# Sampling of a transformer block: one PSUM bank for the takes of both head blocks, output products in halves, another order at the end of the weight stage

## What is computed

```python
v = (value @ w_value + b_value)            # 16 heads of 16
off = (query @ w_off + b_off)              # 4 points of 2 coordinates per head and token
attw = softmax(query @ w_attw + b_attw)    # weights of the 4 points
sx = clip(off[..., 0], 0.0, 1.0); ix = ((sx + 1.0) * L - 1.0) * 0.5
x0 = floor(ix); fx = ix - x0               # between two neighbours of v
sampled = v[x0] * (1 - fx) * ... + v[x0 + 1] * fx * ...
out = einsum('bhlpd,bhlp->blhd', sampled, attw)
x = x + out @ w_out + b_out
```

## Time and profile before

| | us |
|---|---|
| median of 3 runs | 1006.85 |
| lowest, highest | 1002.65, 1007.42 |
| the profiled execution, its own time | 1004.41 |
| its span | 1002.6 |
| mean granted TensorE clock in it | 0.932 of full speed |

### The profile page before, as it was taken

The page is one execution under the profiler, slowest core; times in us unless marked ns, Lnnn a source line. Parts: engine busy times, 40 slices in busy tenths (PEclk is TensorE's granted clock), DMA queues, the critical chain, the costliest instruction groups (busy, mean ns, idle before and its releaser), DMA issues.

```text
span 1002.6 us, 12939 instructions
## 1 busy us (share of the span) xinstructions
PE 838.5 (84%) x4501; PEld 539.6 (54%) x4501; DVE 684.9 (68%) x1237; ACT 539.4 (54%) x1009; POOL 306.0 (31%) x236
## 2 busy tenths in 40 slices
PE   4999998799999998788888899599998994005998
PEld 3776675577777886244444444344443441004887
DVE  2567767866775676579888888735534999895333
ACT  2444434455334665666666666134428995982432
POOL 2100000566110222587777778200010431000000
PEclk9999999799999999599999999799998997556999
DMA  9800000010000000000000000000002436710111
GB/s 290 256 1 1 1 1 1 0 55 0 2 11 1 1 1 1 0 2 1 1 1 1 2 1 2 1 0 1 0 1 84 168 146 275 262 71 11 53 52 53
DMA packets 23446, 45.41 MB, mean 45 GB/s; under 512 B 2323, under 2 KB 18646, under 8 KB 22230
## 3 DMA queue, kind: packets, MB, share of 16 engines
q1 hardware_dynamic: 21776, 43.08, 12.1%
q10 hardware_dynamic: 1606, 1.52, 0.5%
HBM read 27.80 MB, written 16.78 MB: 44 GB/s over the span
## 4 chain that ended last, share of the span: by engine, by line
PE 60%; DVE 20%; POOL 8%; ACT 6%; issue 5%; ACTq 1%; DMA 0%; DVEq 0%; POOLq 0%
PE pair L1313 8%; PE pair L1272 8%; POOL hat L596 5%; PE pair L967 5%; PE pair L1194 4%; PE pair L1075 3%; PE pair L1102 3%; PE pair L1208 3%; PE pair L971 3%; DVE peak L1758 2%; DVE wide L1753 2%; DVE peak L1743 2%; DVE wide L1781 2%; PE pair L1012 2%; PE pair L1104 2%
## 5 line engine op out<-in xcount | busy, mean ns | idle before, releaser
L596 POOL TENSOR_TENSOR hat<-hat 128x1024 f32<-128x1024 f32 x62 | 145.6, 2360 | 45.1 <-DVE hat L1619 44.4
L1178 PE MATMUL pair<-rows,sel 32*128 32x512 bf16 x256 | 75.4, 397 | 23.1 <-ACT down_b L816 17.3
L1619 DVE SCALAR_TENSOR_TENSOR hat<-pair,down_a 128x1024 f32<-128x1024 f32 x64 | 78.1, 1220 | 21.8 <-PE pair L1170 19.7
L1297 PE MATMUL pair<-xqs,wuT 128*128 128x512 f32 x192 | 85.9, 610 | 4.8 <-ACT up_stage L861 4.8
L816 ACT ACTIVATE down_b<-pair 128x512 f32<-128x512 f32 x128 | 69.4, 595 | 37.0 <-PE pair L1178 32.1
L816 ACT ACTIVATE down_a<-pair 128x512 f32<-128x512 f32 x128 | 69.5, 595 | 33.5 <-PE pair L1178 24.0
L1313 PE MATMUL pair<-wdT,hid 128*128 128x256 f32 x384 | 84.8, 384 | 2.9 <-DVE hid L1800 2.9
L1619 DVE SCALAR_TENSOR_TENSOR hat<-pair,down_b 128x1024 f32<-128x1024 f32 x64 | 78.0, 1219 | 11.9 <-PE pair L1170 11.7
L1272 PE MATMUL pair<-xqs,wgT 128*128 128x512 f32 x192 | 85.1, 601 | 0.0
L1313 PEld LDWEIGHTS pair<-wdT,hid 128*128 128x128 f32 x384 | 74.1, 193 | 13.5 <-DVE hid L1800 3.2
L513 POOL TENSOR_TENSOR rstd<-lnt,half 128x8 f32<-128x8 f32 (+2 forms) x15 | 26.5, 1769 | 167.5 <-DVE lnt L1354 167.5
(11 more groups left out here) (208 smaller groups left out, 1880.8 us busy)
## 6 DMA issues: line engine op xcount, KB each, us to landing
up_far<-up_stage SPq DMA_DIRECT2D x24, 512.0 KB, 2.6
ups<-up_far SPq DMA_DIRECT2D x8, 1536.0 KB, 6.7
x_sb<-in_x_dram SPq DMA_DIRECT2D x8, 512.0 KB, 8.2
c_sb<-in_ctx_dram SPq DMA_DIRECT2D x8, 512.0 KB, 9.0
out_dram<-x_sb SPq DMA_DIRECT2D x16, 256.0 KB, 2.1
four<-in_c_four_dram SPq DMA_DIRECT2D x1, 1280.0 KB, 5.7
deq<-in_L_ffn_w_gate_dram SPq DMA_DIRECT2D x1, 768.0 KB, 6.8
deq<-in_L_ffn_w_up_dram SPq DMA_DIRECT2D x1, 768.0 KB, 8.5
```

The source lines that it names most:

```text
L596: nc.gpsimd.tensor_tensor(hat[:, n % RING, :], hat[:, (n - 2) % RING, :], hat[:, n % RING, :], ALU.add).then_inc(summed, 1)
L1178: mm(bank[6 + i], sel[g:g + 32, pp, 1, :], rows[g:g + 32, q, c * 2 + a, :], start=True, stop=True).then_inc(down_mm, 1)
L1297: last = mm(bank[2 + oc], wuT[:, c, oc * 128:(oc + 1) * 128], xqs[:, t % 2, c, :], start=(c == 0), stop=(c == DC - 1))
L1619: V.scalar_tensor_tensor(hat[:, n % RING, :], pair[n % 2][:].rearrange("p i t -> p (i t)"), 0.0, down[n % 2][:].rearrange("p i t -> p (i t ...
```

## The change

- A third buffer for the falling sides (down_c); ScalarE's Relu waits for the hat of three tiles back instead of two.
- Both head blocks accumulate in bank 4. Bank 5 holds only output products. Each clear, apart from the very first, waits until the block before it has been copied.
- The output products are issued in four halves, by head block, at t = 6, 8, 10 and 12. A new semaphore, left_used, tells ScalarE when the c = 0 half of attT is free.
- VectorE's additions move to t = 8 and 13, moments to 9 and 14, ends to 10, 11, 14 and 15.
- At the end of the weight stage TensorE turns the parts of a tick before the value products of that tick, ScalarE goes in the order exponent, rows, second part, first part, and its first two copies of v63 move by two ticks.
- `keep_busy` issues matmuls whose result nobody reads: 6 before and 10 after turn_w63, 6 after the last tick, and 24 behind the last output products.

```diff
--- before.py
+++ after.py
@@ -337,7 +337,7 @@
         w63m = sb("w63m", [QUAD * H, QUAD, L], F32, sample)
         hat = sb("hat", [128, RING, 2 * QUAD * L], F32, sample)
         down_b = sb("down_b", [128, 2, QUAD * L], F32, sample)
-        down = [down_a, down_b]
+        down = [down_a, down_b, sb("down_c", [128, 2, QUAD * L], F32, sample)]
         sample.close()
         lay1.close()
 
@@ -390,6 +390,7 @@
         attT_copied, out_mm, x3_done, vz_clear, vz_ready = (
             sem("attT_copied"), sem("out_mm"), sem("x3_done"), sem("vz_clear"), sem("vz_ready"))
         parts_clear, summed = sem("parts_clear"), sem("summed")
+        left_used = sem("left_used")
 
         def at_seq(b):
 
@@ -797,12 +798,12 @@
                     act.wait_ge(sel_ready, 1)
                 nth(t, S5, copy_tr3)
                 nth(t, S5 + 1, keep_v)
-                if t == S5 + B + 1:
+                for tick, step in ((2, exponent), (10, keep_rows), (7, second_part), (5, first_part)):
+                    if group_at(t, tick) is not None:
+                        step(group_at(t, tick))
+                if t == S5 + B + 3:
                     keep_v63(0)
                     keep_v63(1)
-                for tick, step in ((10, keep_rows), (7, second_part), (2, exponent), (5, first_part)):
-                    if group_at(t, tick) is not None:
-                        step(group_at(t, tick))
                 if t == S5 + B + 5:
                     keep_v63(2)
                     keep_v63(3)
@@ -811,9 +812,9 @@
             def sample_act(n):
                 for i in range(2):
                     act.wait_ge(down_mm, 2 * n + i + 1)
-                    if n >= 2:
-                        act.wait_ge(hat_done, n - 1)
-                    nc.scalar.activation(down[n % 2][:, i, :], bank[6 + i], ACT.Relu).then_inc(down_done, 1)
+                    if n >= 3:
+                        act.wait_ge(hat_done, n - 2)
+                    nc.scalar.activation(down[n % 3][:, i, :], bank[6 + i], ACT.Relu).then_inc(down_done, 1)
                 if n >= TURN and n % TURN == 4:
                     keep_attT(n // TURN - 1, 1)
                 if n % TURN == 12:
@@ -821,9 +822,9 @@
 
             def keep_attT(q, c):
                 act.wait_ge(taken, q * 8 + c * 4 + 4)
-                if c == 0 and q:
-                    act.wait_ge(out_mm, 2 * q)
-                nc.scalar.activation(attT[:, c, :], bank[4 + c][:], ACT.Copy).then_inc(attT_copied, 1)
+                if q:
+                    act.wait_ge(out_mm if c else left_used, 2 * q if c else q)
+                nc.scalar.activation(attT[:, c, :], bank[4], ACT.Copy).then_inc(attT_copied, 1)
 
             for n in range(PAIRS):
                 sample_act(n)
@@ -1130,6 +1131,11 @@
                     last = mm(o, ctx63[:, c, p * 2 * QUAD * H:(p + 1) * 2 * QUAD * H], wval_sb[:, c, :], start=False, stop=(c == DC - 1))
                 last.then_inc(v63_mm, 1)
 
+            def keep_busy(n, place):
+
+                for _ in range(n):
+                    mm(place, idn16[:], rows[:, 0, 0, :], start=True, stop=True)
+
             def turn_w63():
 
                 pe.wait_ge(w63_ready, NG)
@@ -1155,13 +1161,19 @@
                     turn_gw(GW_TICKS.index(t))
                 nth(t, S5, turn3)
                 nth(t, S5 + 1, project3)
+                if t == S5 + B + 6:
+                    pe.wait_ge(v_kept, B)
+                    pe.wait_ge(off_kept, B)
+                    keep_busy(6, bank[3])
+                    turn_w63()
+                    keep_busy(10, bank[3])
+                if group_at(t, 9) is not None:
+                    turn_parts(group_at(t, 9))
                 if t == S5 + B + 1:
                     for p in range(NQ // 2):
                         values63(p)
-                if t == S5 + B + 6:
-                    turn_w63()
-                if group_at(t, 9) is not None:
-                    turn_parts(group_at(t, 9))
+            keep_busy(6, bank[3])
+
             def up_sides(n):
                 if n >= 2:
                     pe.wait_ge(hat_done, n - 1)
@@ -1191,33 +1203,35 @@
                         for i in range(2):
                             q, c, r, pp, a, m, g = tile_of(tile, i)
                             h = c * 128 + 32 * m
-                            last = mm(bank[4 + c][32 * m:32 * m + 32, b * 128:(b + 1) * 128], vz[:, r, b, h:h + 32],
+                            last = mm(bank[4][32 * m:32 * m + 32, b * 128:(b + 1) * 128], vz[:, r, b, h:h + 32],
                                       hat[:, tile % RING, i * QUAD * L + b * 128:i * QUAD * L + (b + 1) * 128],
                                       start=False, stop=(k % 4 >= 2 and tile == n and b == QUAD - 1), skip_group_check=True)
                 last.then_inc(taken, 1)
 
 
-            def project_att(q, i):
-                pe.wait_ge(attT_copied, 2 * q + 2)
-                if i:
-                    pe.wait_ge(x3_done, 2 * q + 1)
-                mm(bank[5][:].rearrange("p (b d) -> p b d", b=2), ones3,
-                   bias3[:, BAT["bout"]:BAT["bout"] + D].unsqueeze(1).broadcast_to([3, 2, D]), start=True, stop=False)
+            def project_att(q, i, c):
+
+                if c == 0:
+                    pe.wait_ge(attT_copied, 2 * q + 2)
+                    if q or i:
+                        pe.wait_ge(x3_done, 2 * q + i)
+                    mm(bank[5][:].rearrange("p (b d) -> p b d", b=2), ones3,
+                       bias3[:, BAT["bout"]:BAT["bout"] + D].unsqueeze(1).broadcast_to([3, 2, D]), start=True, stop=False)
                 for b in range(2):
-                    for c in range(DC):
-                        last = mm(bank[5][:, b * D:(b + 1) * D], attT[:, c, (2 * i + b) * L:(2 * i + b + 1) * L], wout_sb[:, c, :],
-                                  start=False, stop=(b == 1 and c == DC - 1))
-                last.then_inc(out_mm, 1)
+                    last = mm(bank[5][:, b * D:(b + 1) * D], attT[:, c, (2 * i + b) * L:(2 * i + b + 1) * L], wout_sb[:, c, :],
+                              start=False, stop=(c == DC - 1 and b == 1))
+                if c:
+                    last.then_inc(out_mm, 1)
+                elif i:
+                    last.then_inc(left_used, 1)
 
             def clear_att(q, c):
+
                 if c == 0:
                     pe.wait_ge(edge_ready, 2 * q + 2)
-                if q:
-                    pe.wait_ge(attT_copied, 2 * (q - 1) + c + 1)
-                    if c == 1:
-                        pe.wait_ge(x3_done, 2 * q)
-
-                mm(bank[4 + c], v63m[:, c * 128:(c + 1) * 128], w63m[:].rearrange("p b t -> p (b t)"),
+                if q or c:
+                    pe.wait_ge(attT_copied, 2 * q + c)
+                mm(bank[4], v63m[:, c * 128:(c + 1) * 128], w63m[:].rearrange("p b t -> p (b t)"),
                    start=True, stop=True).then_inc(edge_used, 1)
 
             def sample_pe(n):
@@ -1229,8 +1243,8 @@
                     clear_att(q, t // 8)
                 if n >= 5 and n % 2 == 1:
                     take((n - 5) // 2)
-                if q and t in (6, 10):
-                    project_att(q - 1, t // 10)
+                if q and t in (6, 8, 10, 12):
+                    project_att(q - 1, t // 10, (t - 6) // 2 % 2)
 
             pe.wait_ge(w63_kept, 2)
             pe.wait_ge(rows_kept[0], 2 * NG)
@@ -1240,9 +1254,13 @@
                 sample_pe(n)
             take(SUMS - 2)
             take(SUMS - 1)
-            project_att(NQ - 1, 0)
-            project_att(NQ - 1, 1)
-
+            for c in range(DC):
+                project_att(NQ - 1, 0, c)
+            for c in range(DC):
+                project_att(NQ - 1, 1, c)
+
+            pe.wait_ge(hat_done, PAIRS)
+            keep_busy(24, bank[3])
             pe.wait_ge(attT_copied, 2 * NQ)
 
 
@@ -1617,16 +1635,16 @@
                 if n >= RING:
                     dve.wait_ge(taken if n % 4 >= 2 else summed, (n - RING) // 4 * 2 + n % 2 + 1)
                 V.scalar_tensor_tensor(hat[:, n % RING, :], pair[n % 2][:].rearrange("p i t -> p (i t)"), 0.0,
-                                       down[n % 2][:].rearrange("p i t -> p (i t)"), ALU.max, ALU.min).then_inc(hat_done, 1)
+                                       down[n % 3][:].rearrange("p i t -> p (i t)"), ALU.max, ALU.min).then_inc(hat_done, 1)
                 q, t = n // TURN, n % TURN
-                if q and t in (7, 11):
-                    add_out(q - 1, t // 11)
-                if q and t in (8, 12):
-                    two_moments(q - 1, t // 12)
-                if q and t in (9, 10):
-                    two_ends(q - 1, 0, t - 9)
-                if q and t in (13, 15):
-                    two_ends(q - 1, 1, t // 15)
+                if q and t in (8, 13):
+                    add_out(q - 1, t // 13)
+                if q and t in (9, 14):
+                    two_moments(q - 1, t // 14)
+                if q and t in (10, 11):
```

(3 more changed lines are left out.)

## The result

The changed kernel takes 994.2 us (median of 4, 990.59 to 995.97) against 1007.13 for the kernel before (1002.65 to 1021.22, 4 executions): ratio 0.9881, 95% interval [0.9858, 0.9904]. I had forecast 986 in 978 to 994. Direction and place are right, the size isn't: 12.9 us came instead of the 19.65 of my sum. The execution profiled after took 994.94, its span is 993.1.

The account below looks back on a forecast made before the run. It saw the loop as a relay: VectorE binds where its side work is bunched, TensorE and GpSimd elsewhere. Gains of 4.85 + 3.5 + 10.2 + 0.4 + 0.7 = 19.65 took 1004.4 to 984.8 us; forecast 986, range 978 to 994.

Parts of the forecast that it names:

- Step 1: Weight stage's end: turning parts ahead of the value products, with full clock in the last turn, starts the loop 4.85 us earlier.
- step 2: Fillers at the weight stage's end, 6 + 10 + 6 matmuls, lie in waits and cost nothing.
- Step 3: First quad of the loop runs at full clock: gain 3.5 us, bounds 0 and 3.5.
- Step 4: Output products in halves fill TensorE's waits in the loop: 1.7 us a quad over 6 periods, gain 10.2.
- Step 5: One bank for the takes: clears wait for ScalarE's copy, cost 0, from above 5 us.
- Step 6: Third Relu buffer: ScalarE's 0.2 us waits for VectorE go, but it then waits for TensorE; worth nothing.
- Step 7: Last quad: gains 1.6 us up to tile 14, loses 1.2 to moments and ends there; gain 0.4.
- step 8: Tail: 24 fillers hidden ahead of spread_peak speed only the first transposes; gain 0.7 us, bounds 0 and 2.2.
- A: Rival: VectorE binds the second half of each quad, gain only 0.7 us a quad; 992 us, chance 0.20.
- C: Rival: clock falls before the ten weight-stage fillers; 3.5 us lost, 2 to 3 added; 992 us, chance 0.06.
- B: Rival: the clock holds through the tail, a further 1.5 us gained; 984.5 us, chance 0.11.
- D: Rival: one bank serialises take, copy and clear at positions 4 and 13; slower, 1021 us, chance 0.05.

Follow-up runs that it names:

- no_fill: The changed kernel without any of its 46 filler matmuls; 998.05 us, ratio 0.992 to the kernel before.
- loop_fill: The changed kernel with more fillers in the loop: quad 0 at odd tiles and tiles 2 and 4, other quads at tiles 15, 1 and 3; 994.25 us.
- fill_all: The kernel of loop_fill with fillers in the tail too, behind the first spread_peak and the first 8 transposes; 992.4 us, ratio 0.9875.
- quad0_heavy: The changed kernel with three bf16 fillers between the sides of tiles 0 to 5 of quad 0 alone; 993.12 us.
- quad0_fp32: The changed kernel with two float32 products of weight matrices at each of tiles 0 to 5 of quad 0; 992.73 us.
- best: The changed kernel plus three fillers at tiles 0 to 5 of quad 0, two at tiles 15 and 1 of other quads, and tail fillers; 990.71 us.
- after: The changed kernel itself, first measurement and profile; median 994.2 us, profiled execution 994.94, ratio 0.9881 to the kernel before.
- after_timed: The changed kernel, no edit, timed on one chip beside loop_fill and fill_all; 994.25 us.
- after_beside: The changed kernel, no edit, timed on one chip beside tail_fill, quad0_heavy and quad0_fp32; 994.93 us.
- tail_fill: The changed kernel with added fillers in the tail alone, 9 behind the first spread_peak and 1 behind each of the first 8 transposes; 993.13 us.
- after_again: The changed kernel, no edit, profiled a second time; 992.9 us.
- before_again: The kernel before, no edit, profiled a second time; 1020.63 us.
- after_pair: The changed kernel, no edit, timed as the pair of best on its chip; median 996.17 us, profiled execution 1006.06.
- two_buffers: The changed kernel with two Relu buffers instead of three; 1011.18 us, ratio 1.0104 to the kernel before.

## Why the prediction was wrong in size

*Step 1 (order) and step 2 (fillers there)* held: 5.24 measured for 4.85. no_fill parts the two: the order gives 4.88 (21.17 less 16.29), where the sum had 3.95, and full clock in the last turn and behind it 0.36, where it had 0.9. The ten fillers cost nothing: the turn starts 0.05 behind GpSimd's part (404.39) with them and 0.06 without.

*Step 3 (first quad at full clock) is the step that failed:* 3.5 forecast, 0.89 measured. I took it that full clock at the loop's start stays. It fell 3 to 5 us behind the loop's first product in all twelve profiles that entered the loop at full clock and had no fillers in these tiles, or only the fewer ones of loop_fill and fill_all, whatever else was changed in the loop; in the three with two or three full-height products at each of tiles 0 to 5 (quad0_heavy, quad0_fp32, best) it didn't. So it is shown that TensorE's work in these tiles makes the difference. What it is in this work that counts isn't. My lower bound of 0 was right to be there, my choice of the upper one wrong. Nor does any run show that full clock is worth 3.5 there.

*Step 4 (halves)* had the period right: 25.70 measured, 25.6 forecast; six periods gave 9.5 of 10.2, each step within 0.2. What it put at nothing, without a reason, is half clock inside the later quads: 4.2 us in the profiled execution, the largest single part of the miss there. From quad 2 to 6 a quad of 26.9 or 29.9 stands in six of the ten profiles that have this loop without fillers (after, after_timed, after_beside, tail_fill, quad0_heavy, no_fill), in none of the three with fillers in these quads, and in none of the four that keep 27.3. That fits the same cause, but with these numbers it isn't proven. after_again has no such quad and still took 992.9, since its loop began 2.9 later.

*Step 5 (one bank)* held: 0.46 for the copy, covered by GpSimd's sum; with two banks the clear at tile 13 stands 2.30.

*Step 6 (third buffer, "nothing") was wrong:* 0.93 us a quad. I read its value off the old loop, where ScalarE waited 0.2 for VectorE; once the side work is bunched against split products, ScalarE with two buffers waits up to 1.29. It doesn't touch the sum, since the kernel has the buffer, but without it more than half of step 4's gain would be gone.

*Step 7* held (0.35 for 0.4), *step 8* too (1.0 for 0.7). The clock fell at 636.9 among the transposes, as the row at 123.0 suggested, behind two stretches in which TensorE stood, 1.00 us ahead of `spread_peak` and 2.27 behind it. I had read the Trainium skill's "TensorE: Matmul & The Clock Gate" (Part 1) so that the fillers would carry full clock to the gate products; but it also says that idling brings the throttle back, and with that half the trace agrees. I hadn't counted the 2.27, though the same wait stands in the profile of before. With nine fillers in that gap and one behind each of the first eight transposes the clock stayed (tail_fill, 10.46).

Of the rivals, A and C (992 both) came nearest to the number, and by luck. In A's favour, VectorE does bind the second half of each quad (14.11 of 14.44 us), but the first half gave more than it took, and quads are at 25.70, not 26.6. C (fillers cold) had the right suspect in the wrong place: the fillers ran at full clock, the fall came behind them. B, D and E didn't come. The rest of the miss is this execution's: 2.08 ahead of GpSimd's part, where full clock came 5.5 us later at the start of the program, and 1.2 behind the gate products. No step had a term for either. Of the 10.1 between 984.8 and 994.94, then, 2.6 are step 3, 4.2 half clock in quad 3, 3.3 the execution's, and 0.0 the other steps together. The range's upper end, 994, was set from the steps' bounds and left out half clock in the later quads; with the 4.2 of quad 3 it would have been 998.

## What to carry to other kernels

- A chain worked out step by step from one quad's rows gave the new period to 0.1 us. What it can't give is the clock: forecast the loop's time twice, with every quad at full clock and with one of them at a mean clock of 0.83, as in the profile above, and set the range by both.
- A buffer's worth is to be read in the new schedule, not in the old: with whole products the third one was worth 0.05 us a quad together with the one bank, with split products 0.93 alone.
- Fillers cost time even where the engine waits: in the three profiles with four or six of them in a quad, quads 2 to 6 had no half clock and took 0.3 us more than 25.7.
- Look at the mean clock of every execution, not only at the profiled one: it told that the fillers of best do what they are there for, where the times alone left it open.

## What the runs showed that I had not expected

- TensorE fell to half clock (at 411.6) while it was 88 to 90% busy by the profile (the windows from 408 to 412), with the sides' 32-row products alone in hand, and rose again (at 418.4) after the clear, the first take and more sides.
- Half clock can last under steady work: before_again stayed there for 61 us and after_pair for 48, into the middle of quad 1 (quads 0 and 1: 33.7 and 32.3, 33.3 and 32.3 us), with TensorE 90% busy or more in the windows of before_again. The two took 14 and 12 us more than the medians of their kernels.
- A version that does the same work with more waiting loses twice: two_buffers should have cost 6 x 0.93 = 5.6 us and cost 17 against the changed kernel; in its profile three quads with half clock in them lost another 4.6 to 5.2 each.
